# Second FFN of a four-layer token model on one core: dense experts against sorted token-expert tiles

## The chip, the core and the metric

The program runs on one core of a Trainium2 chip. The core has a matrix engine (TensorE, PE in the profile; PEld is its weight load), a vector engine (VectorE, DVE), an activation engine (ScalarE, ACT), a general engine (GpSimd, POOL) and a queue engine (SyncE, SP). They work on a memory of 128 partitions (SBUF); matmuls write to eight banks of PSUM, 128 x 512 floats each. The metric is the device time of one execution in microseconds (us), lower is better.

## The reference, cut to what matters

Eight images of 256 x 256 go through a wavelet step, an attention, a first FFN, a second attention and a second FFN. After the wavelet step there are 2304 tokens of 256 numbers. The second FFN is what the change touches:

```python
xf = layernorm(h)                                   # 2304 x 256
scores = sigmoid(xf @ gate_w.T + lb_bias)           # 2304 x 8
topw, topi = top_k(scores, 2); topw = topw / topw.sum(-1)
for e in range(8):
    m = topi == e; sel = m.any(-1)
    wmean = (topw * m).sum() / max(m.sum(), 1)      # one number for each expert
    y = mlp(xf, gate[e], up[e], down[e])            # 256 -> 128 -> 256, silu(g) * u
    out = out + where(sel, y * wmean, 0)
out = out + mlp(xf, shared_gate, shared_up, shared_down)   # 256 -> 256 -> 256
h = h + out
```

A token counts for two of eight experts, and all tokens for the shared one, which has twice the width and is handled as two halves of 128.

## The kernel before

The residual stream `h` stays in SBUF, 128 partitions x `NT` = 18 tiles x 256. Tokens go in `NG` = 6 groups of three tiles (`GW` = 384 tokens). Every matmul of the FFN is split in three: each float32 operand is a high part in the matmul's own format and a low rest, and high x high, low x high and high x low are added (`split3`, lines 1263 to 1265). The normalised tokens, transposed, lie as `xTh` and `xTl` (256 features x 2304 tokens), the weights as `W_h[1]` and `W_l[1]`; PS is PSUM.

The second FFN is `experts(1, 3)` on four engines. It is dense: ten experts (eight and the two shared halves) run over all six groups, 60 steps n. A step is, in order:

- PE `gate_up(n)`: 12 matmuls with 384 columns into banks 0/1 (gate) and 2/3 (up). It waits for `mul(n-2)`.
- ACT: `sg` = silu(gate) (line 660); DVE `gated(n)`: `aa` = `sg` x up (line 1095); ACT: `ah` = high part of `aa` (line 664); DVE `low(n)`: `al` = rest (line 1101).
- PE `down(n)`: nine matmuls with 256 columns. On PE's queue it stands behind `gate_up(n+1)`, so that the chain above runs beside that.
- DVE `accumulate(n)` (line 1116): three operations `h` = `h` + `cmb` x PSUM, where `cmb` is the expert's mean weight for a chosen token and 0 for another.

Ahead of it the router's logits are in bank 7; DVE's `compare(1)` and `weigh(1)` rank the eight scores of each token and count chosen tokens and weights over a partition (`tot`), PE adds these over the partitions with a matmul with ones (line 1433), and `average()` makes `cmb`. After each group's ten experts SP writes three tiles of `h` out (line 399). POOL has nothing to do in this stage. Each engine runs its own list of instructions in the order of the code, waits on semaphores, and nothing is rescheduled.

Ahead of the FFN a stage of six turns adds the attention's output to `h`, normalises it to `xnp` (two buffers, line 770) and transposes it.

## Time and profile before

| | us |
|---|---|
| median of three runs (881.36 to 884.1) | 882.18 |
| span of the profiled execution | 878.1 |
| attention, first FFN and all else up to the first matmul of the second FFN | 677.25 |
| second FFN, from there to the end of the span | 200.85 |

The profile is of one execution on the one core. Its span goes from the first to the last instruction; what lies around it in the measured time is the difference, 4.1 us against the median. Times within rows are from the span's start. The matmul rows overlap each other (each row's duration has the pipeline's latency in it), so the pace of matmuls is the distance of their starts, not their duration.

### The profile page before, as it was taken

The numbers are of one execution on the slowest core, as the hardware profiler recorded it, in microseconds if no ns is written. First come the engines' busy times: TensorE is split into PE (matmuls) and PEld (weight loads), VectorE is DVE, ScalarE is ACT, GpSimd is POOL, SyncE is SP. The second block draws the span as 40 slices with busy tenths as digits, with TensorE's granted clock in tenths as the row PEclk, the third lists the DMA queues.
The fourth block names the chain that finished last, engine by engine and source line by source line (L and its number), as shares of the span: only waits on it lengthen the run. The fifth ranks groups of instructions, "written<-read, shape, count | busy, mean of one in ns | idle before, by whom it ended". The sixth has DMA issues, their size and how long they took to land.

```text
span 878.1 us, 14320 instructions
## 1 busy us (share of the span) xinstructions
PE 735.0 (84%) x4732; PEld 617.8 (70%) x4732; DVE 614.6 (70%) x1388; ACT 346.6 (39%) x608; POOL 173.5 (20%) x143
## 2 busy tenths in 40 slices
PE   4008997889999999337999999999757899999997
PEld 1007996689999999226655555654545899999997
DVE  6497666677777777927676777673695777777776
ACT  0223554523333333110666666677246233333332
POOL 5623555000000000536112112211253000000000
...
GB/s 252 174 162 1 1 0 0 1 0 2 1 1 1 0 0 0 1 78 81 94 74 76 102 103 89 104 44 23 186 0 1 1 19 1 19 20 1 19 19 19
DMA packets 22246, 38.87 MB, mean 44 GB/s; under 512 B 6972, under 2 KB 17916, under 8 KB 21248
## 3 DMA queue, kind: packets, MB, share of 16 engines
...
q14 instruction: 23, 0.19, 0.1%
...
## 4 chain that ended last, share of the span: by engine, by line
PE 70%; DVE 14%; DMA 6%; issue 3%; ACT 3%; ACTq 2%; POOL 1%; SPq 1%; DVEq 0%; POOLq 0%
PE PS L1263 16%; PE PS L1265 16%; PE PS L1264 16%; PE PS L1541 6%; PE PS L1480 5%; PE PS L1498 4%; DMA wd<-in_wd 2%; DVE MX L1184 2%; DMA KS<-scrH 1%; DVE nmr L1250 1%; ACTq L549 1%; DVE stats L896 1%; PE PS L1323 1%; PE PS L1357 1%; DMA x_in<-in_x 1%
## 5 line engine op out<-in xcount | busy, mean ns | idle before, releaser
L1184 DVE TENSOR_REDUCE MX<-PS 128x1 f32<-128x288 f32 x288 | 125.1, 452 | 52.3 <-PE PS L1480 48.7
L1116 DVE SCALAR_TENSOR_TENSOR h<-PS,cmb,h 128x256 f32<-128x256 f32 (+1 forms) x342 | 143.7, 475 | 0.2 <-PE PS L1265 0.2
L692 ACT ACTIVATE PR<-PS 96x768 f32<-96x768 f32 x144 | 115.3, 806 | 47.8 <-PE PS L1498 44.7
L660 ACT ACTIVATE sg<-PS 128x384 f32<-128x384 f32 x114 | 55.9, 491 | 166.9 <-PE PS L1265 166.9
L1480 PE MATMUL PS<-KS,QS 96*128 96x288 f32 x288 | 97.7, 362 | 18.1 <-DMA KS<-scrH 15.9
L1101 DVE TENSOR_TENSOR al<-aa,ah 128x384 fp32r<-128x384 f32 x114 | 63.6, 558 | 67.2 <-ACT ah L664 67.2
L1480 PEld LDWEIGHTS PS<-KS,QS 96*128 96x128 f32 x288 | 57.6, 204 | 60.3 <-DVE MX L1184 38.7
L664 ACT ACTIVATE ah<-aa 128x384 fp32r<-128x384 f32 x114 | 60.0, 527 | 84.1 <-DVE aa L1095 84.1
L1095 DVE TENSOR_TENSOR aa<-sg,PS 128x384 f32<-128x384 f32 x114 | 63.3, 555 | 27.6 <-ACT sg L660 26.7
L1265 PE MATMUL PS<-xTl,W1h 128*128 128x384 f32 x240 | 81.0, 337 | 0.0
L1263 PE MATMUL PS<-xTh,W1h 128*128 128x384 f32 x240 | 80.8, 337 | 0.0
L1264 PE MATMUL PS<-xTh,W1l 128*128 128x384 f32 x240 | 80.7, 336 | 0.0
L1498 PE MATMUL PS<-QS,KS 128*96 128x384 f32 x288 | 75.9, 348 | 2.1 <-DVE MX L1184 1.1
L1263 PE MATMUL PS<-xTh,W0h 128*128 (+1 forms) x216 | 73.5, 340 | 0.0
L1265 PE MATMUL PS<-xTl,W0h 128*128 (+1 forms) x216 | 73.5, 340 | 0.0
L1264 PE MATMUL PS<-xTh,W0l 128*128 (+1 forms) x216 | 73.4, 340 | 0.0
L1541 PE MATMUL PS<-PR,VA 128*32 128x288 f32 x768 | 66.3, 418 | 1.1 <-ACT yr L746 1.0
L1263 PE MATMUL PS<-W1h,ah 128*128 128x256 f32 x180 | 51.2, 284 | 4.3 <-DVE al L1101 4.3
L1265 PE MATMUL PS<-W1l,ah 128*128 128x256 f32 x180 | 51.0, 283 | 0.0
L1264 PE MATMUL PS<-W1h,al 128*128 128x256 f32 x180 | 50.6, 281 | 0.0
L1263 PE MATMUL PS<-W0h,ah 128*128 128x256 f32 x162 | 46.5, 287 | 4.6 <-DVE al L1101 4.6
L1498 PEld LDWEIGHTS PS<-QS,KS 128*96 128x96 f32 x288 | 42.5, 166 | 9.9 <-ACT PR L692 4.8
...
## 6 DMA issues: line engine op xcount, KB each, us to landing
...
W1raw<-in_w SPq DMA_DIRECT2D x1, 3840.0 KB, 13.2
...
out_tokens<-h SPq DMA_DIRECT2D x6, 384.0 KB, 2.3
```

The lines of the kernel that those rows point to most:

```text
L664: A_(ah[:, b], aa[:, b], ACT.Copy).then_inc(s[f"f{L}_ah"], 1)
L692: A_(PR[0:KT, c0:c0 + 2, :], PS[0:KT, b:b + 2, 0:CW], ACT.Exp).then_inc(s["e_exp"], 1)
L1095: V.tensor_tensor(aa[:, b], sg[:, b], PS[:, 2 + b, 0:GW], ALU.mult).then_inc(s[f"f{L}_mul"], 1)
L1101: V.tensor_tensor(al[:, b], aa[:, b], ah[:, b].bitcast(F32), ALU.subtract).then_inc(s[f"f{L}_al"], 1)
L1116: ins = V.scalar_tensor_tensor(out=hj, in0=PS[:, b + t // 2, (t % 2) * D:(t % 2) * D + D], scalar=cmb[:, ds(g * GT + t, 1), e:e + 1].squee ...
L1184: V.tensor_reduce(MX[:, c // NSH, c % NSH:c % NSH + 1], PS[:, max_bank(it, c), 0:POS], AX_X, ALU.max).then_inc(s["e_mx"], 1)
L1263: M(out_, wh, xh, start=(start and c == 0), stop=False)
L1264: M(out_, wl, xh, start=False, stop=False)
L1265: ins = M(out_, wh, xl, start=False, stop=(stop and c == n - 1))
L1480: M(PS[:, max_bank(it, c), 0:POS], QS[q][0:MROW, c * P:c * P + P], KS[q][0:MROW, c // 9 * POS:c // 9 * POS + POS], start=True, stop=True). ...
L1498: ins = M(PS[0:KT, n % 4, 0:CW], KS[p][:, g * POS + kt * KT:g * POS + kt * KT + KT], QS[p][:, g * HQ + cc * CW:g * HQ + cc * CW + CW], sta ...
L1541: ins = M(PS[32 * hh:32 * hh + 32, 6, 0:POS], VA[p][:, kt, g, :], PR[:, c0:c0 + 3, :].rearrange("p c w -> p (c w)")[:, hh * POS:hh * POS + ...
```

## The change

The eight experts of the second FFN are no longer dense. A token has two chosen experts, so there are 4608 token-expert pairs. They are sorted by expert into tiles of 128 slots, each expert's last tile padded: `NTL` = 36 + 7 = 43 tiles always suffice and all 43 are run.

- While the first shared half (six dense steps) runs on PE, DVE works out the slot of each pair and from that the two index lists: `scan_counts`, `tile_bases`, `token_slots`, `one_hot_tiles`, `one_hot_rows` (three parts), `indices`, `tile_experts`. The lists are turned from slots by 36 matmuls of one-hot matrices between `gate_up(4)` and `down(2)`. `tile_experts` gives each tile's expert (PE loads these 43 numbers into registers and takes its weights by them) and the mean weight `wt`.
- In the stage ahead SP also writes `xnp` to the DRAM tensor `scrX`, six DMAs of 384 KB.
- Tile t: POOL gathers 128 rows of 1 KB from `scrX` with an indirect DMA into `xg` (four buffers); PE transposes them (`x_turn`, 2 matmuls), ACT and DVE make the high and low part (`x_high`, `x_low`), PE runs gate and up together with the tokens as weights (`a_gate_up`, 6 matmuls with 256 columns), ACT `a_silu`, DVE `a_gated`, PE `a_turn` (1 transpose), ACT `a_high`, DVE `a_low`, PE `a_down` (3 matmuls with 256 columns), ACT `y_out` (times `wt`, into `ysb`, four buffers), and POOL scatters the 128 rows into the DRAM tensor `scrY` by pair, with another indirect DMA.
- Then the second shared half runs (six dense steps), SP reads `scrY` back in six DMAs of 768 KB into `yb`, POOL adds the two rows of each token (`pair_sum`), DVE adds them and the shared half to `h` (`last_add`, `last_pair`), and SP writes `h` out at the end.
- In the dense steps the low part is made by POOL (`dense_low`), and the first half's result goes over ACT (`dense_out` to `ysh`) and POOL (`dense_add`) into `h`.
- Four small constant tables are loaded at the program's start by SP. Semaphores of the earlier stages are shared and get offsets; nothing else of these stages changes.

The core of the diff (the functions of the index lists are left out; their operations stand below by engine order):

```diff
+NTL = TOK * 2 // P + NE - 1
+NTP = (NTL + 1) // 2 * 2
+NXG, NXS, NYS = 4, 3, 4
+NDS = 2 * NG
...
-        with sp.Fori(0, NG) as g:
-            sp.wait_ge(s["f1_acc"], 10 * (g + 1))
-            sp.dma_start(out[:, ds(g * GT, GT), :], h[:, ds(g * GT, GT), :]).then_inc(s["d_out"], 16)
+        for g in range(NG):
+            sp.wait_ge(s["n_xn"], N0["p"] + g + 1)
+            sp.dma_start(scrX[g * GW:(g + 1) * GW, :].rearrange("(t p) d -> p t d", p=P), xnp[:, g % 2]).then_inc(s[f"d_xo{g % 2}"], 16)
+        for b in range(NYS):
+            sp.wait_ge(s[f"d_ys{b}"], 16 * len(range(b, NTL, NYS)))
+        for g in range(NG):
+            if g >= 4:
+                sp.wait_ge(s["m_ya"], g - 3)
+            sp.dma_start(yb[:, g % 4], scrY[2 * g * GW:2 * (g + 1) * GW, :].rearrange("(t p k) d -> p t (k d)", p=P, k=2)).then_inc(s[f"d_yb{g % 4}"], 16)
+        for g in range(NG):
+            sp.wait_ge(s["f1_out"], g + 1)
+            sp.dma_start(out[:, g * GT:(g + 1) * GT, :], h[:, g * GT:(g + 1) * GT, :]).then_inc(s["d_out"], 16)
...
+        def dense_low(n):
+            pool.wait_ge(s["f_ah"], F0[1, "ah"] + n + 1)
+            wait(pool, s["f_dn"], F0[1, "dn"] + n - 1)
+            nc.gpsimd.tensor_tensor(al[:, n % 2], aa[:, n % 2], ah[:, n % 2].bitcast(F32), ALU.subtract).then_inc(s["f_al"], 1)
+        def dense_add(n):
+            pool.wait_ge(s["f1_yc"], n + 1)
+            z = slice(n * GT, n * GT + GT)
+            nc.gpsimd.tensor_tensor(h[:, z, :], h[:, z, :], ysh[:, n % 2], ALU.add).then_inc(s["f_acc"], 1)
+        def gather(t):
+            wait(pool, s["m_xT"], t - NXG + 1)
+            nc.gpsimd.indirect_dma_start(xg[:, t % NXG, :], None, scrX, bass.IndirectOffsetOnAxis(ap=gix[:, t:t + 1], axis=0))\
+                .then_inc(s[f"d_xg{t % NXG}"], 16)
+        def scatter(t):
+            pool.wait_ge(s["m_yo"], t + 1)
+            nc.gpsimd.indirect_dma_start(scrY, bass.IndirectOffsetOnAxis(ap=six[:, t:t + 1], axis=0), ysb[:, t % NYS, :], None,
+                                         bounds_check=TOK * 2 - 1, oob_is_err=False).then_inc(s[f"d_ys{t % NYS}"], 16)
+        def pair_sum(g):
+            pool.wait_ge(s[f"d_yb{g % 4}"], 16 * (g // 4 + 1))
+            nc.gpsimd.tensor_tensor(yb[:, g % 4, :, 0:D], yb[:, g % 4, :, 0:D], yb[:, g % 4, :, D:2 * D], ALU.add).then_inc(s["m_ysum"], 1)
+        for n in range(NG):
+            dense_low(n)
+            if n >= 2:
+                dense_add(n - 2)
+        pool.wait_ge(s["m_idx"], 1)
+        pool.wait_ge(s["d_xo0"], 16 * (NG // 2))
+        pool.wait_ge(s["d_xo1"], 16 * (NG // 2))
+        gather(0)
+        gather(1)
+        dense_add(NG - 2)
+        dense_add(NG - 1)
+        for t in range(2, 5):
+            gather(t)
+        for t in range(NTL):
+            if t + 5 < NTL:
+                gather(t + 5)
+            scatter(t)
+        for n in range(NG, NDS):
+            dense_low(n)
+            if n >= NG + 2:
+                pair_sum(n - NG - 2)
+        pair_sum(NG - 2)
+        pair_sum(NG - 1)
...
+        def x_high(t):
+            act.wait_ge(s["m_xT"], t + 1)
+            wait(act, s["m_gu"], t - NXS + 1)
+            A_(xsh[:, t % NXS], PS[:, 6 + t % 2, 0:D].rearrange("p (k c) -> p k c", k=KC), ACT.Copy).then_inc(s["m_xh"], 1)
+        def a_silu(t):
+            act.wait_ge(s["m_gu"], t + 1)
+            wait(act, s["m_a"], t - 1)
+            A_(sgt[:, t % 2], PS[:, t % 2, 0:P], ACT.Silu).then_inc(s["m_silu"], 1)
+        def a_high(t):
+            act.wait_ge(s["m_aT"], t + 1)
+            wait(act, s["m_y"], t - 1)
+            A_(aht[:, t % 2], PS[:, 2 + t % 2, 0:P], ACT.Copy).then_inc(s["m_ah"], 1)
+        def y_out(t):
+            act.wait_ge(s["m_y"], t + 1)
+            wait(act, s[f"d_ys{t % NYS}"], 16 * (t // NYS))
+            A_(ysb[:, t % NYS], PS[:, 4 + t % 2, 0:D], ACT.Copy, scale=wt[:, t:t + 1]).then_inc(s["m_yo"], 1)
...
+        for i in range(NTL + 2):
+            if i < NTL:
+                a_silu(i)
+            if 1 <= i <= NTL:
+                a_high(i - 1)
+            if i + 2 < NTL:
+                x_high(i + 2)
+            if i >= 2:
+                y_out(i - 2)
+        for n in range(NG, NDS):
+            dense_silu(n)
+            dense_high(n)
...
+        compare(1)
+        weigh(1)
+        scan_counts()
+        gated(0)
+        tile_bases()
+        token_slots()
+        gated(1)
+        one_hot_tiles()
+        one_hot_rows(0)
+        gated(2)
+        one_hot_rows(1)
+        one_hot_rows(2)
+        gated(3)
+        indices()
+        tile_experts()
+        gated(4)
+        gated(5)
+        x_low(0)
+        x_low(1)
+        for i in range(NTL + 1):
+            if i < NTL:
+                a_gated(i)
+            if i >= 1:
+                a_low(i - 1)
+            if i + 2 < NTL:
+                x_low(i + 2)
+        for n in range(NG, NDS):
+            gated(n)
+            if n >= NG + 2:
+                last_add(n - 2)
+            if n >= NG + 3:
+                last_pair(n - NG - 3)
+        last_add(NDS - 2)
+        last_pair(NG - 3)
+        last_add(NDS - 1)
+        last_pair(NG - 2)
+        last_pair(NG - 1)
...
+        def x_turn(t):
+            pe.wait_ge(s[f"d_xg{t % NXG}"], 16 * (t // NXG + 1))
+            wait(pe, s["m_xl"], t - 1)
+            for k in range(KC):
+                ins = nc.tensor.transpose(PS[:, 6 + t % 2, k * P:k * P + P], xg[:, t % NXG, k * P:k * P + P], ident[:, :])
+            ins.then_inc(s["m_xT"], 1)
+        def a_gate_up(t, e):
+            pe.wait_ge(s["m_xl"], t + 1)
+            wait(pe, s["m_a"], t - 1)
+            o_ = PS[:, t % 2, 0:2 * P].rearrange("p (a i) -> p a i", a=2)
+            b = t % NXS
+            for k in range(KC):
+                M(o_, xsh[:, b, k], gu[0][:, :, ds(e + k * P, P)], start=(k == 0), stop=False)
+                M(o_, xsl[:, b, k], gu[0][:, :, ds(e + k * P, P)], start=False, stop=False)
+                ins = M(o_, xsh[:, b, k], gu[1][:, :, ds(e + k * P, P)], start=False, stop=(k == KC - 1))
+            ins.then_inc(s["m_gu"], 1)
+        def a_turn(t):
+            pe.wait_ge(s["m_a"], t + 1)
+            wait(pe, s["m_al"], t - 1)
+            nc.tensor.transpose(PS[:, 2 + t % 2, 0:P], aat[:, t % 2], ident[:, :]).then_inc(s["m_aT"], 1)
+        def a_down(t, e):
+            pe.wait_ge(s["m_al"], t + 1)
+            if t == 0:
+                pe.wait_ge(s["f1_yc"], NG)
+            wait(pe, s["m_yo"], t - 1)
+            o_ = PS[:, 4 + t % 2, 0:D]
+            b = t % 2
+            M(o_, aht[:, b], dn[0][:, ds(e, D)], start=True, stop=False)
+            M(o_, alt[:, b], dn[0][:, ds(e, D)], start=False, stop=False)
+            M(o_, aht[:, b], dn[1][:, ds(e, D)], start=False, stop=True).then_inc(s["m_y"], 1)
+        for n in range(NG):
+            dense_gate_up(n)
+            if n == 1:
+                pe.wait_ge(s["f1_tot"], 1)
+                M(PS[:, 7, 0:2 * NE], ones[:, :], tot[:, :], start=True, stop=True)
+                M(PS[:, 7, 2 * NE:3 * NE], tri[:, :], tot[:, 0:NE], start=True, stop=True).then_inc(s["f1_sum"], 1)
+            if n == 4:
+                for m in range(NT * 2):
+                    if m % (NT * 2 // 3) == 0:
+                        pe.wait_ge(s["m_oh"], m // (NT * 2 // 3) + 1)
+                    ins = M(PS[:, 6, 0:NTP], ohp[:, m], ohv[:, m], start=(m == 0), stop=(m == NT * 2 - 1))
+                ins.then_inc(s["m_ix"], 1)
+            if n >= 2:
+                dense_down(n - 2)
+        dense_down(NG - 2)
+        dense_down(NG - 1)
+        pe.wait_ge(s["m_te"], 1)
+        te = [pe.alloc_register(f"te{t}") for t in range(NTL)]
+        pe.load(te[0:22], tei[0:1, 0:22])
+        pe.load(te[22:NTL], tei[0:1, 22:NTL])
+        te = [pe.snap(r, min_val=0, max_val=(NE - 1) * KC * P) for r in te]
+        x_turn(0)
+        x_turn(1)
+        for i in range(NTL + 2):
+            if i < NTL:
+                a_gate_up(i, te[i])
+            if 1 <= i <= NTL:
+                a_turn(i - 1)
+            if i + 2 < NTL:
+                x_turn(i + 2)
+            if i >= 2:
+                a_down(i - 2, te[i - 2])
+        for n in range(NG, NDS):
+            dense_gate_up(n)
+            if n >= NG + 2:
+                dense_down(n - 2)
+        dense_down(NDS - 2)
+        dense_down(NDS - 1)
```

In the order lists that follow, a row is an instruction: line of the kernel, operation, output<-inputs, shape, and the semaphores that it waits for.

DVE at the start of the second FFN, before. `ra` are comparisons of scores, t_135 to t_137 the ranks and weights, `sv` the normed weights:

```order
L1045 TENSOR_TENSOR ra<-sc 128x18
L1095 TENSOR_TENSOR aa<-sg,PS 128x384 [waits f1_silu,dve_own]
L1101 TENSOR_TENSOR al<-aa,ah 128x384 [waits f1_ah]
L1050 TENSOR_REDUCE t_135<-ra 128x144
L1052 TENSOR_SCALAR t_136<-t_135 128x144 [waits dve_own]
L1054 TENSOR_TENSOR t_137<-t_136,sc 128x144 [waits dve_own]
```

And with the change, from the end of `token_slots` to the start of `indices`:

```order
L1504 CAST tpf<-tpi 128x72 [waits dve_own]
L1542 TENSOR_TENSOR aa<-sg,PS 128x384 [waits f_al,f_silu,dve_own]
L1509 TENSOR_TENSOR oht<-tpf,cst 128x1584
L1512 TENSOR_TENSOR ohv<-oht,vid 128x1584 [waits dve_own]
L1518 TENSOR_TENSOR ohp<-tpf,iot 128x1536 [waits dve_own]
L1542 TENSOR_TENSOR aa<-sg,PS 128x384 [waits f_al,f_silu]
L1518 TENSOR_TENSOR ohp<-tpf,iot 128x1536 x2
L1542 TENSOR_TENSOR aa<-sg,PS 128x384 [waits f_al,f_silu]
L1524 COPY ixf<-PS 128x43 [waits m_ix]
```

The gating of the first step (line 1095, now 1542) stood right behind the comparisons; now the gating operations of steps 0 to 5 stand spread over the whole index work, up to four of its large operations between two of them.

POOL after the last low part of the weights. Before, its list ends there:

```order
L413 TENSOR_TENSOR rstd<-mt,minus_half 128x3 [waits var_ready]
L537 TENSOR_TENSOR W1l<-W1raw,W1h 128x1280 [waits w_hi1]
L413 TENSOR_TENSOR rstd<-mt,minus_half 128x3 [waits var_ready]
L537 TENSOR_TENSOR W1l<-W1raw,W1h 128x1280 [waits w_hi1] x2
L1590 UNCONDITIONAL_BRANCH
```

With the change, from the last dense step of the first half on (rows of line 626 are gathers, of 632 scatters):

```order
L615 TENSOR_TENSOR al<-aa,ah 128x384 [waits f_dn,f_ah]
L621 TENSOR_TENSOR h<-h,ysh 128x768 [waits f1_yc]
L626 DMA xg<-scrX,gix 128x256 [waits d_xo1,d_xo0,m_idx]
L626 DMA xg<-scrX,gix 128x256
L621 TENSOR_TENSOR h<-h,ysh 128x768 [waits f1_yc] x2
L626 DMA xg<-scrX,gix 128x256 x2
L626 DMA xg<-scrX,gix 128x256 [waits m_xT] x2
L632 DMA scrY<-ysb,six 4608x256 [waits m_yo]
L626 DMA xg<-scrX,gix 128x256 [waits m_xT]
L632 DMA scrY<-ysb,six 4608x256 [waits m_yo]
L626 DMA xg<-scrX,gix 128x256 [waits m_xT]
L632 DMA scrY<-ysb,six 4608x256 [waits m_yo]
```

So gather t+6 stands right behind scatter t on one in-order queue, and scatter t waits for `y_out(t)`.

PE in the experts' part, before (the last three of a dense step's 12 gate-and-up matmuls and the first three of the nine `down` matmuls behind them):

```order
L1263 MATMUL PS<-xTh,W1h 128x384
L1264 MATMUL PS<-xTh,W1l 128x384
L1265 MATMUL PS<-xTl,W1h 128x384
L1263 MATMUL PS<-W1h,ah 128x256 [waits f1_acc,f1_al]
L1264 MATMUL PS<-W1h,al 128x256
L1265 MATMUL PS<-W1l,ah 128x256
```

With the change, the end of one tile turn (after its six gate-and-up matmuls, of which the last three stand here) and the first row of the next:

```order
L1997 MATMUL PS<-W1h,xsh 128x256
L1998 MATMUL PS<-W1h,xsl 128x256
L1999 REGISTER_ALU
L1999 MATMUL PS<-W1l,xsh 128x256
L2006 MATMUL PS<-ident,aat 128x128 [waits m_al,m_a]
L1987 MATMUL PS<-ident,xg 128x128 [waits m_xl,d_xg1]
L1987 MATMUL PS<-ident,xg 128x128
L2016 ISA [waits m_al]
L2016 MATMUL PS<-W1h,aht 128x256
L2017 MATMUL PS<-W1h,alt 128x256
L2018 REGISTER_ALU
L2018 MATMUL PS<-W1l,aht 128x256
```

In turn i PE runs the gate and up of tile i, the inner transpose of tile i-1, the transpose of the gathered rows of tile i+2 (it waits for that gather's landing, `d_xg1` here) and the down matmuls of tile i-2.

## Rows read from the trace of the kernel before

**Rows 1.** The page: busy time by engine; DMA rate in 40 slices of the span.

```profile
PE 735.0 (84%) x4732; PEld 617.8 (70%) x4732; DVE 614.6 (70%) x1388; ACT 346.6 (39%) x608; POOL 173.5 (20%) x143
...
GB/s 252 174 162 1 1 0 0 1 0 2 1 1 1 0 0 0 1 78 81 94 74 76 102 103 89 104 44 23 186 0 1 1 19 1 19 20 1 19 19 19
```

**Rows 2.** Timeline of the second FFN, its ends: start, duration, engine, line, operation.

```profile
677.25 0.44 PE L1263 MATMUL PS<-xTh,W1h 128*128 128x384 f32 x1
...
872.55 0.38 PE L1263 MATMUL PS<-W1h,ah 128*128 128x256 f32 x1 [1.25 <-DVE al L1101]
...
875.37 0.34 SPq L399 DMA_DIRECT2D out_tokens<-h  x1
```

**Rows 3.** The same view, one dense step and a pair of its down matmuls.

```profile
775.96 0.34 PE L1263 MATMUL PS<-xTh,W1h 128*128 128x384 f32 x1
...
778.17 0.28 PE L1264 MATMUL PS<-W1h,al 128*128 128x256 f32 x1
...
778.29 0.28 PE L1265 MATMUL PS<-W1l,ah 128*128 128x256 f32 x1
...
779.13 0.34 PE L1263 MATMUL PS<-xTh,W1h 128*128 128x384 f32 x1
```

**Rows 4.** Busy time by stretch, 720 to 875 us: length, PE, PEld, DVE, ACT, POOL, clock.

```profile
720.00:875.00 155.00, 152.63 (x1012) 152.22 (x1010) 112.45 (x247) 48.87 (x96) 0.00 (x0) 1.00 0.03 12
```

**Rows 5.** Timeline, DVE's router work at the start of the second FFN.

```profile
678.58 0.31 DVE L1045 TENSOR_TENSOR ra<-sc 128x144 f32<-128x144 f32 x1 [0.92 <-ACT sc L650]
...
680.96 0.55 DVE L1095 TENSOR_TENSOR aa<-sg,PS 128x384 f32<-128x384 f32 x1
...
686.14 0.40 DVE L1071 TENSOR_REDUCE tot<-sv 128x8 f32<-128x144 f32 x1
```

**Rows 6.** Groups by shape on DVE: line, output<-inputs, shapes, count | busy us, mean ns.

```profile
L1095 DVE TENSOR_TENSOR aa<-sg,PS 128x384 f32<-128x384 f32 x60 | 33.3, 555 | 16.7 <-ACT sg L660 16.1 <-DVE tot L1071 0.5
L1239 DVE TENSOR_TENSOR h<-PS,h 128x768 f32<-128x768 f32 x6 | 5.7, 950 | 4.3 <-PE PS L1570 4.3
L1067 DVE TENSOR_TENSOR sv<-t,t 128x144 f32<-128x144 f32 x1 | 0.3, 309 | 0.0
```

**Rows 7.** Groups by shape on ACT, as in rows 6.

```profile
L746 ACT ACTIVATE yr<-PS 128x288 f32<-128x288 f32 x32 | 13.0, 406 | 1.0 <-PE PS L1541 1.0
L709 ACT ACTIVATE VA<-PS 96x64 f32<-96x64 f32 x24 | 3.5, 220 | 0.5 <-PE PS L1512 0.5
```

**Rows 8.** Groups by shape on POOL, as in rows 6.

```profile
L450 POOL TENSOR_TENSOR qs<-qsq 128x384 f32<-128x384 f32 x6 | 6.0, 1004 | 43.9 <-ACT qsq L591 43.9
L464 POOL TENSOR_TENSOR a1l<-a1raw,a1h 128x768 fp32r<-128x768 f32 x1 | 1.9, 1902 | 4.8 <-ACT a1h L671 4.8
L413 POOL TENSOR_TENSOR rstd<-mt,minus_half 128x3 f32<-128x3 f32 x6 | 5.1, 855 | 25.8 <-DVE mt L798 25.8
L438 POOL TENSOR_TENSOR rwl<-rw,rwh 128x16 fp32r<-128x16 f32 x2 | 3.5, 1777 | 0.0
```

**Rows 9.** The DMA view: tensors, issuing queue, count, KB each, us to landing.

```profile
recb<-scrR ACTq DMA_DIRECT2D x56, 36.0 KB, 1.9
...
W1raw<-in_w SPq DMA_DIRECT2D x1, 3840.0 KB, 13.2
...
out_tokens<-h SPq DMA_DIRECT2D x6, 384.0 KB, 2.3
```

**Rows 10.** Timeline, six transposes at full clock.

```profile
117.74 0.82 PE L1292 MATMUL PS<-ident,xn 128*128 128x128 f32 x6
```

**Rows 11.** Busy time by stretch of 4 us, as in rows 4 (PE first, clock third from the end).

```profile
640.00:644.00 4.00, 0.07 (x1) 0.08 (x2) 3.72 (x14) 3.44 (x5) 0.91 (x2) 0.87 0.00 0
644.00:648.00 4.00, 4.00 (x14) 2.83 (x15) 3.97 (x3) 1.14 (x3) 2.80 (x1) 0.50 0.00 0
684.00:688.00 4.00, 2.54 (x15) 2.12 (x13) 3.22 (x12) 0.37 (x1) 0.00 (x0) 1.00 0.00 2
```

**Rows 12.** The chain that ended last, at the program's start: start, length, what.

```profile
21.86 21.89 DMA wd<-in_wd
```

337 lines of the change are left out of this document (276 added, 61 removed).

## Prediction

> **What bounds the kernel now.** I read the page's busy line first, then the timeline of the second FFN, then its groups. PE is busy 84% of the span [rows 1], and in the stretch that the change rewrites it never rests: from 720 to 875 us it is busy 152.6 of 155 us at full clock, DVE 112 us, ACT 49 us, POOL not at all [rows 4]. One dense step takes 779.13 - 775.96 = 3.17 us of PE [rows 3]; DVE's and ACT's work of a step is shorter and lies beside it. 60 steps make 190 us of the 200.85 us from the first gate matmul at 677.25 to the end of the span at 878.1 [rows 2]; the rest is router work at the head and the last chain and store at the end. So matmul columns bound this stage, and the change removes columns: 48 of 60 dense steps, 48 x 3.17 = 152 us. What it puts there is bound by other things, and the question is by what.
>
> **The work of a tile.** Matmuls of 256 columns start 0.12 us apart (778.17, 778.29) [rows 3]; a transpose of 128 columns takes about 0.11 us ((0.82 - 0.16) / 6 [rows 10]; 0.16 is what a matmul's duration has over its distance, 0.28 - 0.12 [rows 3]). A tile has nine such matmuls and three transposes: 9 x 0.12 + 3 x 0.11 = 1.4 us of PE at full clock, 60 us for 43 tiles. ACT has two operations of 128 and two of 256 columns. Between 64 columns (220 ns) and 288 (406 ns) a column costs 0.83 ns [rows 7], so these take 0.27 and 0.38 us, 1.3 us in all. DVE has two of 128 and one of 256: between 144 (309 ns) and 384 (555 ns) it is 1.0 ns a column [rows 6], 0.3 + 0.3 + 0.42 = 1.0 us. Each chain is staggered over turns. If nothing but these engines counted, a turn would be about 1.5 to 1.6 us, half of a dense step, though 43 turns replace 48 steps.
>
> **POOL and the transfers set the turn.** A turn also has one gather and one scatter on POOL's in-order queue. The trace has no indirect DMA. Its nearest rows bound what POOL spends on one, D. From below it is SP's issue of a plain 128-partition transfer, 0.34 us [rows 2]. From above I take the longest of POOL's small operations, 1.78 us for 16 columns; the power on three columns takes 0.86 us [rows 8]. Working out 128 addresses is a loop on this engine like these, not a fixed issue like SP's, so I take the mean of 0.86 and 1.78, **D = 1.3 us**. From issue to landing a plain transfer takes 1.9 us for 36 KB from DRAM and 2.3 us for 384 KB to it [rows 9]; for 128 KB I take 2.1 less the issue, 1.8 us after POOL is done.
>
> Now the loop. Gather t+6 stands behind scatter t, scatter t waits for `y_out(t)`, that for the down matmuls at the end of PE's turn t+2; and gather t+6 must have landed for `x_turn(t+6)` in PE's turn t+4. So two turns hold: 0.6 us from PE's last matmul to the end of `y_out` (0.2 latency, 0.38), 2D = 2.6 for scatter and gather, 1.8 for the landing, 0.6 for the transposes and the down matmuls that end turn t+4. That is 5.6 us, **2.8 us a turn**. POOL's own bound, 2D = 2.6, is just under it; PE's 1.4 is hidden. Four buffers for gathered rows and four for results don't bind earlier: in 4 x 2.8 us both transfers are long over. In general the turn is T = max(2D, D + 1.5).
>
> The Trainium skill (DMA: Bandwidth & Descriptors, Anatomy of one DMA) puts a GpSimd-issued transfer at 2.0 us and its bytes over 436 GB/s, 2.3 us here from end to end; with that instead of D + 1.8 a turn would come to 2.4 us (0.6 + 1.3 for the scatter + 2.3 + 0.6, halved) and the total 14 us lower. No transfer of this kind is in this trace.
>
> **The head, 677.25 to 730 us.** Without the change DVE does the comparisons from 678.58, gates step 0 at 680.96, and ends the weighing at about 686.5 [rows 5]. Now comparisons (2.4 us), weighing (4.0) and the scan (0.7) stand ahead of `gated(0)`, which ends at 686.2; PE can run only two gate-and-ups ahead and stands. Behind it DVE has `tile_bases` (2.2 us: nine operations of 0.16 to 0.31 us with waits between them), `token_slots` (2.3), a gating (0.56), five one-hot operations of 1536 or 1584 columns (1.8 each by 1.0 ns a column and 0.2, so 9.0), two gatings, the wait for PE's last 12 index matmuls (1.3), `indices` (1.5) at 703.6, `tile_experts` (3.0) and the last gatings to 707.7. PE then has the last down matmuls, whose low parts come from POOL at 1.0 us each [rows 8]: done at about 712. This is 35 us for six dense steps that take 19 on their own: 16 us of index work that nothing covers. The indices are ready at 703.6 but POOL reaches gather 0 only behind the low part of step 5 and an add of 768 columns (1.9 us) [rows 8], at 711.6; two gathers (2.6), two more adds (3.8), then gathers 2, 3, 4 at 1.3 each, and the transposed rows of tiles 2 to 4 come one by one as they land, 721 to 724. Scatter 0 and gather 6 follow at 726.2 and 727.5, and turn 4 ends at **730**. So the head, with turns 0 to 4 in it, takes 53 us.
>
> **The loop.** Turns 5 to 40 wait for gathers: 36 x 2.8 = 101 us. The last four wait for none: 1.5 each, 6 us. It ends at 837.
>
> **The tail.** Six dense steps at 3.17 are 19 us, and the last gating, high part, low part (on POOL now) and down matmuls stand alone: before, PE idled 1.25 us ahead of them at 872.55 and they ran 1.2 [rows 2]; with POOL and its waits 3.5 us in all. Then a `last_add` and two `last_pair` at 0.95 [rows 6] and the store, 2.7 us from 875.37 to the end [rows 2]: 28 us. Beside it run the last scatters (landed 3.4 us behind the last turn) and six loads of 768 KB. 3840 KB take 13.2 us [rows 9], so one takes 2.6 at that pace, the last lands at 20.5, its pair sum (1.9), add and store end at 26. This is just hidden; 10% slower loads would show. End at 865.
>
> **Small parts.** The stage ahead writes `xnp` to DRAM: a 384 KB store lands in 2.3 us [rows 9] and a buffer comes round only each second group, so nothing waits; SP has nothing urgent behind it. If it were not hidden it would cost at most 2.3 us a group, 14 us. At the start SP gets four more loads, 290 KB, that share the engines with weight loads on the chain, `wd` to 43.75 us [rows 12]: about 1.2 us at the 252 GB/s of the first slice [rows 1]. That half of `h`'s updates now go over ACT and POOL costs nothing: both have under 3 us a step of 3.17.
>
> **Sum.** 865 + 1.2 = 866 us of span against 878.1, 12 us less. Around the span lie 4.1 us (882.18 - 878.1), kept: **870 us**.
>
> **Rivals.**
> - *POOL's queue becomes the bound and loses more than PE gains* (slower). Head and tail are fixed, so the change breaks even at T = 2.8 + 12 / 36 = 3.1 us; by T = max(2D, D + 1.5) from D = 1.6 us on. At the row of 1.78 us it is 3.56, 27 us above the forecast: 897 us. For it: the upper row is a plain operation on far less data. Against: the pow row. Chance 0.20.
> - *Cheap issues.* With D = 0.7, twice SP's issue [rows 2], T is 2.2 and the end 36 x 0.6 = 22 us earlier: 848 us. At D = 0.34 the bound is 1.84 and the total 835. Chance 0.19.
> - *The clock falls in the loop.* After a stretch with 0.07 us of PE work in 4 us the granted clock went to 0.50; with 2.54 of 4 us it stayed at 1.00 [rows 11]. PE stands nearly idle from 712 to 721, so the tiles start at half of 2.4 GHz, where a turn is 2.8 us of PE and no longer hidden; at 1.4 of 2.8 us busy it may stay there, which adds the doubled transposes and downs to the loop: (5.6 + 0.6) / 2 = 3.1 us a turn, 11 us more, no gain left, 881 us. That row's busy share, 64%, lies above the loop's 50%, so this is open. Chance 0.13.
> - *Gathers and scatters don't overlap* (slower). If each must land before the next is served, a turn is 2 x (1.3 + 1.8) = 6.2 us: 36 x 3.4 = 122 us more, 992 us. Nothing in the code orders the two kinds, so this has 0.03. The Trainium skill speaks for large transfers (DMA: Bandwidth & Descriptors, Rules for kernel authors: at least 1 MiB per DMA; under 64 KB mostly overhead); these are 128 KB.
>
> **Chances and range.** The forecast, D from 1.1 to 1.5 and with it T from 2.6 to 3.0, has 0.45 and spans 862 to 878 us. Faster by over 0.3% (under 879.5; 0.3% is about what a measurement tells from no change) are the forecast, the cheap issues and a third of the clock's case: 0.68. Within 0.3% are the rest of the clock's case and a little of the first rival: 0.10. Slower: 0.22. The range reaches from D = 0.5 (T = 2.0, 841) to T = 3.45 (893): 840 to 893 us.
>
> **What would show it right or wrong.** In the changed kernel's trace: starts of `a_gate_up` 2.8 us apart and PE's waits in `x_turn` ended by the DMA into `xg`; POOL's DMA rows near 1.3 us; turn 4 over at 730, first gather at 711 to 712, loop's end at 837; PE stopped behind line 1542 in the head. If PE's waits are ended by POOL's queue with no gap on POOL, it is the 2D bound; if POOL's rows are 1 us or less, the cheap case. The forecast is wrong if a first use of the indirect DMA costs more than the later ones, or if `yb` loads of 2 KB rows are slower than weight loads.

## Result

The changed kernel takes 904.53 us (median of 4 runs, 903.03 to 910.2) where the one before takes 881.85: ratio 1.0254, 95% interval 1.0224 to 1.0283. Forecast were 870 us, range 840 to 893, slower with 0.22. It is slower, by 23 us, and outside the range. The profiled execution has a span of 903.7 us, 37.5 more than my sum of 865 + 1.2.

The page of the changed kernel, answering to [rows 1]:

```profile
PE 688.0 (76%) x4278; PEld 557.6 (62%) x4278; DVE 555.4 (61%) x1276; ACT 358.7 (40%) x690; POOL 298.5 (33%) x253
...
PEclk9999999899999998566999999998968677888787
...
PE 52%; DVE 17%; DMA 12%; issue 7%; POOL 5%; ACT 4%; ACTq 1%; SPq 1%; DVEq 0%; POOLq 0%
```

The same two lines of the kernel before, the clock and the chain of work that ended last:

```profile
PEclk9999998889999999556899999999978999999999
...
PE 70%; DVE 14%; DMA 6%; issue 3%; ACT 3%; ACTq 2%; POOL 1%; SPq 1%; DVEq 0%; POOLq 0%
```

PE has 47 us less to do than before, and the span is 26 us longer: what left the matmuls came back as DMA and "issue" in the chain, and TensorE's granted clock is lower in the last quarter. The stage in stretches of 15 us (length, PE, PEld, DVE, ACT, POOL, clock), answering to [rows 4]:

```profile
745.00:760.00 15.00, 9.22 (x58) 8.00 (x58) 4.15 (x14) 6.05 (x20) 9.33 (x10) 0.84 0.24 76
760.00:775.00 15.00, 12.59 (x57) 11.06 (x56) 4.14 (x13) 5.96 (x18) 8.64 (x9) 0.51 0.24 75
775.00:790.00 15.00, 7.91 (x58) 6.70 (x57) 4.36 (x15) 6.29 (x20) 9.85 (x10) 1.00 0.26 84
```

No engine is full, and the stretch at half clock (0.51) gets about as many matmuls done (57) as the one at full clock (58). So PE's work does not set the loop's time, though its clock has a share in it, told of below. The chain of waits shows whose it is. One round of it (start, length, what):

```profile
844.62 0.48 ACT ysb L941
845.10 0.02 issue
845.13 0.03 POOLq L632
845.15 0.74 issue
845.90 1.02 POOL scrY L632
846.91 0.31 issue
847.22 2.72 DMA xg<-scrX,gix
849.94 0.04 issue
849.99 0.69 PE PS L1987 x2
850.67 0.21 PE PS L2016
850.89 0.21 PE PS L2017
851.10 0.23 PE PS L2018
851.33 0.02 issue
851.35 0.48 ACT ysb L941
```

This is the cycle that the prediction described: `y_out(t)`, scatter t, gather t+6, its landing, `x_turn(t+6)`, the down matmuls, `y_out(t+2)`. It takes 851.35 - 844.62 = 6.73 us for two turns, 3.36 a turn, where I had 5.6 and 2.8. From gather 6 (740.5) to gather 42 (861.6) the 36 turns took 3.36 us each.

### The profile page after: what moved, and what is told of

Read it like the earlier page. It is cut to its first block, busy times and chain, and to the rows that moved or that the text cites. A ratio compares the mean times of both kernels' runs of the same rounds, so it can differ in the third digit from the quotient of the medians.

```text
span 903.7 us, 13928 instructions
## 1 busy us (share of the span) xinstructions
PE 688.0 (76%) x4278; PEld 557.6 (62%) x4278; DVE 555.4 (61%) x1276; ACT 358.7 (40%) x690; POOL 298.5 (33%) x253
## 4 chain that ended last, share of the span: by engine, by line
PE 52%; DVE 17%; DMA 12%; issue 7%; POOL 5%; ACT 4%; ACTq 1%; SPq 1%; DVEq 0%; POOLq 0%
PE PS L1627 9%; PE PS L1629 9%; PE PS L1628 9%; DMA xg<-scrX,gix 6%; PE PS L1905 6%; PE PS L1844 5%; PE PS L1862 4%; DMA wd<-in_wd 3%; POOL scrY L632 2%; DVE MX L1372 2%; DMA KS<-scrH 2%; PE PS L1987 1%; DVE nmr L1438 1%; DVE stats L1084 1%; ACTq L674 1%
## 5 line engine op out<-in xcount | busy, mean ns | idle before, releaser
L1304 DVE SCALAR_TENSOR_TENSOR h<-PS,cmb,h 128x256 f32 (+1 forms) x162 | 68.1, 475 | 0.0
L1987 PE MATMUL PS<-ident,xg 128*128 128x128 f32 x86 | 23.8, 372 | 55.6 <-DMA xg<-scrX,gix 48.4
L1547 DVE TENSOR_TENSOR xsl<-PS,xsh 128x256 fp32r<-128x256 f32 x43 | 18.3, 425 | 72.4 <-ACT xsh L923 72.3
L584 POOL TENSOR_TENSOR recb<-yr,recb 128x1152 f32<-128x1152 f32 x7 | 18.5, 2650 | 128.5 <-DMA recb<-scrR 128.5
L632 POOL DMA_INDIRECT scrY<-ysb,six x43 | 43.6, 1015 | 48.1 <-ACT ysb L941 40.5
L785 ACT ACTIVATE sg<-PS 128x384 f32<-128x384 f32 x54 | 26.5, 491 | 79.1 <-PE PS L1629 79.1
L1987 PEld LDWEIGHTS PS<-ident,xg 128*128 128x128 f32 x86 | 11.5, 179 | 65.1 <-DMA xg<-scrX,gix 57.7
L1289 DVE TENSOR_TENSOR al<-aa,ah 128x384 fp32r<-128x384 f32 x54 | 30.2, 558 | 32.1 <-ACT ah L789 32.1
L626 POOL DMA_INDIRECT xg<-scrX,gix x43 | 42.1, 980 | 12.8 <-issue 11.0
L1629 PE MATMUL PS<-W0l,ah 128*128 128x256 f32 x162 | 45.9, 283 | 0.0
```

The lines of the kernel that those rows point to most:

```text
L626: nc.gpsimd.indirect_dma_start(xg[:, t % NXG, :], None, scrX, bass.IndirectOffsetOnAxis(ap=gix[:, t:t + 1], axis=0))\
L632: nc.gpsimd.indirect_dma_start(scrY, bass.IndirectOffsetOnAxis(ap=six[:, t:t + 1], axis=0), ysb[:, t % NYS, :], None, bounds_check=TOK * 2 ...
L1304: ins = V.scalar_tensor_tensor(out=hj, in0=PS[:, b + t // 2, (t % 2) * D:(t % 2) * D + D], scalar=cmb[:, ds(g * GT + t, 1), e:e + 1].squee ...
L1629: ins = M(out_, wh, xl, start=False, stop=(stop and c == n - 1))
L1987: ins = nc.tensor.transpose(PS[:, 6 + t % 2, k * P:k * P + P], xg[:, t % NXG, k * P:k * P + P], ident[:, :])
```

## Where the 37.5 us are

| piece | predicted | measured | difference |
|---|---|---|---|
| first gate matmul | 677.25 + 1.2 | 679.42 | +1.0 |
| from there to the end of turn 4 | 52.8 | 64.9 (744.3) | +12.1 |
| to the last down matmul | 107 | 125.9 (870.2) | +18.9 |
| to the end | 28 | 33.5 | +5.5 |

**Loop.** The two waits of the cycle, PE's in `x_turn` for the landing and POOL's for `y_out`, from 725 to 850 us (total, times, longest). The forecast had both; they are longer than it had them:

```profile
PE PS L1987 <- DMA xg<-scrX,gix: 43.0, 27, 3.4
POOL scrY L632 <- ACT ysb L941: 32.1, 20, 4.8
```

**Head.** Rows of the timeline, PE, DVE, POOL and PE again:

```profile
687.29 0.61 PE L2024 MATMUL PS<-tot,ones 128*128 128x16 f32 x2 [3.44 <-DVEq L1261]
...
712.07 0.20 DVE L1524 COPY ixf<-PS 128x43 f32<-128x43 f32 x1 [7.20 <-PE PS L2030]
...
723.48 1.19 POOL L626 DMA_INDIRECT xg<-scrX,gix  x1 [0.18 <-issue]
...
730.10 1.11 PE L1987 MATMUL PS<-ident,xg 128*128 128x128 f32 x4 [6.98 <-issue]
```

PE pauses 3.44 us for the totals and 2.6 us ahead of `gate_up(4)`; the clock is 0.50 from 700 to 716 us, so that step takes 4 us and the 36 index matmuls 7.7 us (0.214 apart). The lists are ready at 713.4, forecast 703.6; gather 0 starts 10.1 us behind them, forecast 8.0; and then 7.0 us of PE go to two reads of 22 and 21 registers (the expert offsets, 2.05 and 4.99 us), for which the sum had no term. Counted from the first gate matmul, the 12.1 us over the forecast are 7.6 to the lists, 2.1 from there to gather 0, 1.1 from gather 0 to scatter 0 (15.7 for 14.6) and 1.3 on to turn 4.

**Tail.** Groups from 870 us on, DVE's and POOL's, answering to [rows 6, 8] (after the bar busy us, then mean ns):

```profile
L1575 DVE TENSOR_TENSOR h<-yb,h 128x768 f32<-128x768 f32 x6 | 10.1, 1684 | 1.0 <-POOL yb L638 0.6 <-DVE h L1575 0.2
L1568 DVE TENSOR_TENSOR h<-PS,h 128x768 f32<-128x768 f32 x6 | 5.7, 956 | 0.3
...
L638 POOL TENSOR_TENSOR yb<-yb 128x768 f32<-128x768 f32 x6 | 13.7, 2300 | 0.0
```

and the loads of the pairs, on the page:

```profile
yb<-scrY SPq DMA_DIRECT2D x6, 768.0 KB, 6.1
```

An addition of 768 columns takes DVE 950 ns and POOL 1.9 us alone [rows 6, 8]; with both at work on such additions the mean is 1684 and 2300 ns. Only `last_pair` (L1575, both inputs in SBUF) is slower; `last_add` (L1568, one input in PSUM) stays at 956 ns in the same stretch. A load takes 6.1 us to land, but the next ones run beside it: POOL never stood idle ahead of a sum (0.0), and the last additions wait for POOL's sums and not for a load.

## Experiments

The experiments ran in five groups on five chips, A to E, each chip once. The ratio is always to the kernel before, run beside the others of its group, with its 95% interval. No ratio of the kernels with a lead of 6 or 7 is more than 2% from 1. Where a time stands against one of another chip, the text says so.

### The cycle, by the lead of the gathers

`gather(t + L)` is started ahead of `scatter(t)`; L is 5 in the change. The gather behind scatter t is t+L+1, needed L-3 turns after `y_out(t)`: the cycle's time is spread over L-3 turns.

```
-            if t + 5 < NTL:
-                gather(t + 5)
+            if t + 7 < NTL:
+                gather(t + 7)
```

Lead 7 (chip A) and lead 4 (chip B):

> GpSimd starts gather t+7 instead of gather t+5 ahead of scatter t; nothing else changes. Theory A (the loop runs at a cycle: y_out(t), GpSimd's start on scatter t, gather t+6 behind it, its landing, two tiles later in x_turn): with seven tiles of lead the landing no longer stands in the cycle, the turn falls from 3.36 us toward GpSimd's own two issues with their gaps (1.02 + 0.30 + 0.98 + 0.30 = 2.60 us), the 43 us of waits of x_turn on the gathered rows nearly vanish, and the time falls by about 25 us, to 880. Theory B (the gathers' transfers themselves are slow or the clock sets the turn): the wait stays at x_turn, with later landings, and the time stays within 3 us of the change's.

> The gathers run four tiles ahead in place of five. Cycle theory: one round of y_out, scatter, gather, landing, x_turn to y_out, which spans L - 3 turns at a lead of L (two at 5, over which it measured 6.2 to 6.7 us), now has to fit into one turn: the turn goes from 3.36 to 6.2 to 6.7 us, and the time up by 36 to 38 turns times 3.0 us, to 1010 to 1030. Rival (the loop is bound by transfers, by the clock or by the engines' work in it, and the lead only smooths it): less than 40 us more.

Lead 6 (chip D), after the pauses told of below had been seen:

> The changed kernel with a lead of six as the one edit. Cycle theory: the round of 6.2 to 6.7 us now spans three turns, 2.1 to 2.2 us each, under GpSimd's 2.60, so the turn is 2.60 and the time that of the lead of seven, 870 to 880, if ScalarE makes no pauses. If pauses of ScalarE (1 to 3 us with nothing that the trace shows to wait for, 43 us in all) are the rule once GpSimd's queue runs without a gap, they appear here, and the time is 890 to 900.

| lead | turns in the cycle | us a turn | time, ratio |
|---|---|---|---|
| 4 | 1 | 6.87 | 1041.3, 1.1788 (1.1764 to 1.1811) |
| 5 | 2 | 3.36 | 904.5, 1.0254 |
| 6 | 3 | 2.61 | 877.2, 0.9923 (0.9886 to 0.9960) |
| 7 | 4 | 2.60 | 874.7, 0.9911 (0.9877 to 0.9945) |

At lead 4 the round of the chain is the same 6.77 us, in one turn:

```profile
903.07 0.48 ACT ysb L941
...
904.35 1.01 POOL scrY L632
...
905.67 2.76 DMA xg<-scrX,gix
...
909.84 0.48 ACT ysb L941
```

Half of 6.73 is 3.36; a third would be 2.24, but POOL alone needs 2.60 for a scatter and a gather with the 0.30 us behind each, and from lead 6 on its DMAs follow each other at that distance nearly throughout. Timeline of POOL at lead 7:

```profile
765.48 0.98 POOL L626 DMA_INDIRECT xg<-scrX,gix  x1 [0.30 <-issue]
766.76 1.02 POOL L632 DMA_INDIRECT scrY<-ysb,six  x1 [0.30 <-issue]
768.09 0.97 POOL L626 DMA_INDIRECT xg<-scrX,gix  x1 [0.31 <-issue]
```

Theory A holds: the cycle cost the loop its gain. With the same DMAs and the same work, two tiles sooner in the queue, `x_turn(0)` to the last down matmul takes 107.5 us in place of 140.1, and the kernel comes under the one before, on this chip. (The medians are 30 us apart, across two chips. In that profile the lists were also ready 3.1 us sooner, by the clock in the index matmuls; more of this below.)

### The clock

```
+            wait(pe, s["m_xl"], t - 1)
+            for _ in range(3):
+                M(PS[:, 6 + t % 2, 0:P], ones[:, :], ident[:, :], start=True, stop=True)
             pe.wait_ge(s[f"d_xg{t % NXG}"], 16 * (t // NXG + 1))
-            wait(pe, s["m_xl"], t - 1)
```

> Three idle matmuls of 128 columns are put ahead of each x_turn's wait for its gathered rows, into the columns that the transposes then write; they fill some 0.6 us of the pause of each turn. If the half clock of parts of the loop (mean 0.76 over 730 to 860) is a cause of the long turns of its own, the granted clock rises to about 1 and the turn falls from 3.36 to about 3.1 us, 9 us less in all. If the cycle through GpSimd and the transfer sets the turn whatever the clock, the time changes by under 3 us either way.

```profile
805.00:820.00 15.00, 10.40 (x81) 9.38 (x79) 4.14 (x14) 5.67 (x18) 8.95 (x9) 1.00 0.25 74
```

907.4 us, 1.0280 (1.0249 to 1.0312). The clock was 0.93 to 1.00 from 745 on and the round 6.25 us where it closes (840.75 to 847.00), yet gathers were 3.32 us apart on the mean: a scatter also waits at times behind a gather of POOL's own queue. So at full clock too the loop is far over the forecast's 2.8. The run does not settle the clock's own share, since the added matmuls stand in PE's queue themselves and delay a turn whose rows have landed. The change's own trace bounds it: from 775 to 790 (clock 1.00) four gathers follow at 3.12 us each, from 760 to 775 (clock 0.51) at 3.49. Against the mean of 3.36 the half clock costs up to 0.24 us a turn, an estimate of at most 9 us of the loop.

In the head, with twelve and eight such matmuls in PE's two pauses:

> Twelve idle matmuls in TensorE's pause ahead of the totals (685 to 688) and eight in the one ahead of gate_up(4) (697 to 700). Theory: the half clock of 700 to 715 costs 2 us in gate_up(4) and 3.9 us in the 36 index matmuls, so the lists are ready 5 to 6 us sooner; but gather 0 starts 10 us behind the lists, held by GpSimd's dense_low and adds, so that the kernel gains 3 to 6 us. Rival: an index matmul is bound by its weight load and its interval of 0.214 us stays at full clock; then 2 us or less.

903.3 us, 1.0222 (1.0184 to 1.0261). The clock was 1.00 from 700 to 708 us and the index matmuls took 4.1 us in place of 7.7, so the rival on the weight load falls; first gate matmul to `x_turn(0)` is 46.8 us where it was 50.7. The median moved by 1.2 us, inside both intervals, so that no gain in the time is shown. Nor is the shorter head shown to be the edit's: of the 17 other profiles with the index work, none of them with this edit, ten have the 36 index matmuls in 4.6 to 5.2 us and seven in 7.7, with both kinds on chip B. Lead 4 and lead 7 have 46.9 and 47.5 us to `x_turn(0)` with the head as in the change. The clock of this stretch differs from one execution to another, by some 3 us of the head.

### The head's other pieces

Offsets read one per turn, behind `a_gate_up(i)`, in the change (chip A) and at lead 7 (chip D):

```
-        pe.load(te[0:22], tei[0:1, 0:22])
-        pe.load(te[22:NTL], tei[0:1, 22:NTL])
+            if i + 1 < NTL:
+                pe.load(te[i + 1:i + 2], tei[0:1, i + 1:i + 2])
```

> TensorE reads the expert offset of tile i+1 behind gate_up(i), one register at a time, in place of two reads of 22 and 21 registers ahead of the loop (2.05 and 4.99 us). Theory: gather 0 has landed at 726.5 and x_turn(0) starts at 730.1, so 3.6 us are gained and the loop is unchanged: minus 3.6 us. Rival: each single read costs about a microsecond on TensorE's sequencer in each of the 43 turns; where the pause of the turn hides it, minus 3.6 stays, where not, up to 20 us more.

906.8 us, 1.0252 (1.0219 to 1.0285): nothing gained. Gather 0 to `x_turn(0)` fell from 6.6 to 3.0 us, but to scatter 0 only from 15.7 to 14.6, and the loop from `x_turn(0)` was 2 us longer: turns 2 to 4 wait for gathers that POOL starts late, so that of the 3.6 us some 1.1 stood on the path. That profile's stage ahead also ended 8.6 us later.

> On the kernel with a lead of seven: expert offsets read one per turn, as the one edit. There the two reads stand at the path (dense_down(5) ends at 719.5, x_turn(0) starts at 726.5, gather 0 has landed at 722.8). Theory: x_turn(0) 3.7 us sooner, loop at GpSimd's 2.60 us as before: 871. Rival: this kernel falls into ScalarE's pauses as the five others with a lead of seven: 890 or more; then the one without pauses was the exception and not the order of GpSimd's queue.

870.9 us, 0.9868 (0.9801 to 0.9936). First gate matmul to `x_turn(0)`: 43.4 us, where 47.5 had stood. The medians are 3.8 us apart, across two chips, and that this is the number expected is luck: from `x_turn(0)` to the last down matmul it took 110.6 us for 107.5, so that from the first gate matmul 1.0 us is left of it (154.0 for 155.0), and 3.5 of the 4.4 us between the two spans lie ahead of the second FFN.

Lists that are not computed (the output is another; what is left out stands in the expectation), lead 7, chip C:

> On the kernel with a lead of seven: the counting, the slots, the one-hots, the 36 index matmuls and the tiles' experts are left out; gather and scatter lists are the tokens in order, the expert offset is that of expert 0, and the pair weight 0.5, so the output is another. Everything else stays. Theory (the head's length is that of the list building): VectorE's 15 us of it and the 5 to 8 us of index matmuls go, the dense steps follow each other at about 3.2 us from 687 on, x_turn(0) starts at 706 to 710 in place of 726.5, and the time falls by 17 to 20 us, to 855 to 858. Rival (GpSimd's dense_low and adds, 2.8 us a step and stretched, and the 7 us of register loads set the start): 5 us or less.

884.8 us, 1.0013 (0.9991 to 1.0035), on a chip where lead 7 has the pauses told of next. First gate matmul to `x_turn(0)` is 35.9 us against 47.5 and 50.7 in the two profiles of lead 7: building the lists costs 12 to 15 us on the path, under the 17 to 20 expected, since behind the last dense step the 7.0 us of reads still stand. Against lead 7 with the pauses (1.0101, chip E) the ratio is 0.9 points lower, 8 us.

Gathers 0 and 1 ahead of `dense_low(4)`:

> On the kernel with a lead of seven: gathers 0 and 1 are put ahead of dense_low(4) and (5) in GpSimd's order. In that kernel gather 0 starts 10.3 us behind the last step of the lists. Theory A (the head is late by GpSimd's order): gather 0 starts 1 us behind the lists, but dense_low(4) now waits for the lists too (they are there at 710, dense_low(4) ran at about 715), so nothing is lost there, x_turn(0) starts as soon as TensorE has done dense_down(5) and its register loads, 3 to 5 us sooner: 870. Theory B (x_turn(0) is held by TensorE's dense steps and the 7 us of register loads behind them): within 1.5 us of 874.7.

> Gathers 0 and 1 ahead of dense_low(4) and (5), lead of seven, once more; it had the pauses and took 891. If they belong to the chip, it stands against the lead of seven as the edit alone does: within 1.5 us of it if TensorE's dense steps and register loads hold x_turn(0), 3 to 5 us under it if GpSimd's order does.

On chip B 891.0 us, 1.0069 (1.0034 to 1.0105). On chip E, beside lead 7 without the edit, 894.1 us, 1.0110 (1.0071 to 1.0149), against 894.5; first gate matmul to `x_turn(0)` 50.8 against 50.7: no gain. Theory B holds: 10 us between the lists and gather 0 look long, but `x_turn(0)` waited for PE's own steps and reads.

### The same kernel, 20 us apart on two chips

The run on chip B took 891.0, not 870 to 875, and the next with a lead of 7, on chips B and C, were slow as well. In these, ACT starts operations up to 3.1 us late: ACT's groups, lead 7 on chip A, and the same kernel on chip E (idle time ahead, and what ended it):

```profile
L941 ACT ACTIVATE ysb<-PS,wt 128x256 f32<-128x256 f32 x31 | 14.7, 474 | 0.8 <-PE PS L2018 0.7
L929 ACT ACTIVATE sgt<-PS 128x128 f32<-128x128 f32 x31 | 8.6, 277 | 9.4 <-PE PS L1999 9.4
```

```profile
L941 ACT ACTIVATE ysb<-PS,wt 128x256 f32<-128x256 f32 x27 | 12.9, 479 | 16.3 <-remote 10.3 <-PE PS L2018 5.2 <-issue 0.8
L929 ACT ACTIVATE sgt<-PS 128x128 f32<-128x128 f32 x27 | 7.6, 281 | 20.9 <-PE PS L1999 10.8 <-remote 7.8 <-issue 2.4
```

I call it a pause where an ACT operation starts over 0.3 us after both its PE operation and its predecessor have ended. Summed over the loop, the pauses are 0 to 0.7 us in all profiles at lead 4 or 5 (chips A, B, C among them) and on chips A and D at lead 6 or 7, and 55 to 59 us, 39 to 48 pauses, in the eight at lead 7 on chips B, C and E. Gathers that land long ahead of the loop are one suspect, tried at lead 5:

> The changed kernel itself, lead of five, with gathers 0 and 1 ahead of dense_low(4) and (5) as the one edit. It asks where the pauses of ScalarE come from that lengthened the loop from 107 to 126 us when this edit was made at a lead of seven. If they come with early gathers: ScalarE's unexplained pauses (43 us in all there) appear here too, and the time is 910 or more. If they need GpSimd's queue without a gap (lead of seven): none of them, and 900 to 905.

Chip C: 909.1 us, 1.0275 (1.0256 to 1.0295), no pauses; it is not the early gathers alone. The next two ask for the lead and for the landings that ACT waits for, both on the kernel with two dense steps ahead of the loop, told of below:

> The kernel of the two dense steps ahead of the loop, with a lead of six in place of seven. If ScalarE's pauses hang on how far GpSimd may run ahead, they shrink and the time falls from 888 toward 868; if they hang on a queue without a gap, 885 to 890.

> The kernel of the two dense steps ahead of the loop, lead of seven, with eight output tiles instead of four, so that y_out(t) waits for the landing of scatter t-8 and not t-4. If ScalarE's pauses are waits for landings of scatters, they go and the time falls to about 868; if not, 885 to 890.

Both ran without pauses on chip D, 874.8 us, 0.9874 (0.9815 to 0.9934) and 868.5 us, 0.9834 (0.9766 to 0.9902), and so did the two others on that chip (lead 6, and lead 7 with reads per turn): four kernels without pauses tell nothing of the edits, and point to the chip. By then ten kernels at lead 6 or 7 had run, five with pauses and five without (the next expectation counts one fewer with them). Three kernels unchanged on chip E decide it, of which one had run without pauses and two with:

> The lead of seven once more, unchanged, beside the next two on one chip. So far the eight runs of kernels with a lead of six or seven fall in two groups: five without ScalarE's pauses on two chips (loop 104 to 108 us from x_turn(0) to the last down), four with 43 to 49 us of them on two other chips. If the pauses belong to the chip, the three kernels here are all with, or all without; without them this one comes to 875 again, with them to about 893.

> The kernel of the two dense steps ahead of the loop once more, unchanged; it had the pauses and took 888. If they belong to the kernel, 885 to 890 here whatever the lead of seven beside it does; if to the chip, the same group as the lead of seven: 868 without, 888 with.

Lead 7 unchanged: 894.5 us, 1.0101 (1.0066 to 1.0136), with pauses of 58 us, turn 3.08 us. Two steps: 895.2 us, 1.0119 (1.0087 to 1.0151). The pauses go with the chip (or with what else differed between the five groups, since no chip was used twice) and with POOL's queue at its limit: chips B and C had none at lead 4 and 5. A piece of the timeline of lead 7 on chip E, PE's last gate-and-up matmul of tile 6, and ACT's silu of that tile with the operation before it:

```profile
744.58 0.28 PE L1999 MATMUL PS<-W1l,xsh 128*128 x1
...
745.93 0.47 ACT L941 ACTIVATE ysb<-PS,wt 128x256 f32<-128x256 f32 x1 [0.39 <-remote]
748.81 0.28 ACT L929 ACTIVATE sgt<-PS 128x128 f32<-128x128 f32 x1 [2.40 <-PE PS L1999]
```

What ACT waits for there can be read from the semaphores' updates in the traces. 335 of the 343 pauses end within 0.06 us behind an update of the very semaphore that the tile's own PE operation raises, and none behind a landing that the operation waits for. For tile 6 above the matmul has ended at 744.86 by its row and the update comes at 748.78, 3.9 us later; in the profiles without pauses at lead 6 and 7 it always comes 0.02 us behind the row's end. So ACT does not wait for scatters to land, which the run with eight output tiles, made where no pauses were, could not tell; it waits for PE's signal. Whether the matmul itself ends late (the ends of PE's rows are modelled) or only its signal is late, and why on some chips alone, stays open. At lead 5, where POOL's queue has gaps, chips A and C gave 903 to 909 us.

### The tail, and moving the dense steps

All six dense steps of the second half ahead of the loop, and then in addition both additions of a pair sum on DVE (lead 7, reads per turn, chip B, with pauses):

> On the kernel with a lead of seven, with the offsets read one per turn: the six dense steps of the second shared half move from behind the loop to ahead of it. Theory (the head has 20 to 25 us in which TensorE only waits for the lists, and the tail of 33.5 us is TensorE's 19 us of dense steps beside 17.5 us of transfers at the 400 GB/s that its windows show): the head ends at about 727 in place of 726.5, and the tail shrinks from 33.5 to some 20 us (2 landing of the last scatter, 3 first pair load, 12 to 14 for six pair sums on GpSimd and VectorE, 3 last store): about 860. Rival: VectorE, busy without a break to 704 and with 9.5 us more work (gated and last adds) in the head, pushes the loop's start back by the full 19 us; then 874 or more.

> On the kernel of the shared halves ahead of the loop: VectorE does both additions of a pair sum, and GpSimd none. In the changed kernel's tail GpSimd's pair_sum took 2.30 us and VectorE's last_pair 1.68 us beside it, where such an operation of VectorE alone took 0.95. Theory (the two engines hold each other up over their two inputs): six times 2 x 0.95 = 11.4 us in place of 6 x 2.3 = 13.8 and the 1.7 behind the last, 3 to 4 us less. Rival (the tail then goes by its loads of 768 KB, 4.6 MB at 400 GB/s = 11.5 us): within 1 us.

```profile
L1562 DVE TENSOR_TENSOR yb<-yb 128x768 f32<-128x768 f32 x6 | 5.8, 958 | 11.2 <-DMA yb<-scrY 10.0 <-DVE h L1564 1.2
L1564 DVE TENSOR_TENSOR h<-yb,h 128x768 f32<-128x768 f32 x6 | 5.8, 958 | 0.2
```

902.0 us, 1.0197 (1.0173 to 1.0221), and 901.3 us, 1.0200 (1.0149 to 1.0252). From the last down matmul of the loop to the end the first takes 30.7 us, the second 26.0, with 33.5 in the change: alone, DVE's additions are back at 958 ns, and the 4.7 us are somewhat more than the 3 to 4 expected, though the medians (0.7 apart) don't show them. The steps ahead of the loop gave back 2.8 us in the tail and pushed `x_turn(0)` back by 16.8 us: it starts 60.2 us behind the first gate matmul, where the same kernel with the steps behind the loop has 43.4. The rival, which had the full 19 us, was nearly right. Two steps in place of six, in the 7 us that PE spent on reads:

> On the kernel with a lead of seven: two of the six dense steps of the second half go into TensorE's pause ahead of the loop (7 us there), offsets are read one per turn, four gathers instead of two are started ahead of the last two adds, and VectorE does the pair sums alone. Expected from the rows: loop start as before at about 726.5 (6.4 us of dense work in place of 7.0 us of register loads), the tail 33.5 - 6.4 = 27 us: 868. Rival (the pauses of up to 3 us of ScalarE that stood in the loops with early gathers, 42 us in all, come with any gather that lands long ahead of the loop): 885 or more.

Chip C, 887.7 us, 1.0076 (1.0037 to 1.0114), with pauses. With eight output tiles in place of four, on chip D, it gave the lowest median, 868.5 us, against 870.9 for lead 7 with reads per turn on the same chip: the intervals of the two ratios overlap, so neither is shown to be the faster, and the profiles say why (tail 28.9 in place of 33.6 us, head 48.6 in place of 43.4).

So five versions beat the kernel before on chips A and D, by 0.8 to 1.7%, with every interval under 1. The one of them that was run again elsewhere, lead 7, was 1.0% slower than the kernel before on chip E. None is shown to be faster on every chip.

## Why the prediction was wrong

- **What sets the turn: right.** PE waits in `x_turn`, ended by the DMA into `xg`; POOL has gaps; the cycle has the steps that were named, and the three other leads bear out its form.
- **Its size: wrong, and this is the step that failed.** At full clock a round is 6.25 us, at half clock 6.73, not 5.6. I set D = 1.3 and it is 0.98 and 1.02, so the dear term was cheap (2 D = 2.0 for 2.6), and issue to landing is 2.75 where D + 1.8 gave 3.1. (The estimate of 2.3 us worked out from the Trainium skill, DMA: Bandwidth & Descriptors, Anatomy of one DMA, is 0.45 short. The turn of 2.4 us made from it also lies under the forecast's own bound of 2D = 2.6; by that bound it would have been 7 us less in all, not 14.) What was missing has no busy time in any row of before: 0.80 us from the end of `y_out` to POOL's start on the scatter, 0.31 between two of POOL's DMAs, and 0.85 to 1.34 us of PE in place of 0.6. T = max(2D, D + 1.5) took D for all that POOL does; right is max(2D + 0.6, cycle / (L - 3)). Over the 36 turns the 0.56 us are 20 of the 37.5 us, about 12 of them at full clock already (3.12 for 2.8).
- **Luck.** POOL's own bound came out right, 2.60 us at leads 6 and 7 for 2D = 2.6: a D that was 0.3 too large stood for the gap of 0.3 that the sum had left out.
- **The rivals.** "POOL bound" had the right sign and the wrong cause: D never came near 1.6. But its break-even, a turn of 3.1 us, was passed: the turn was 3.36. The clock did fall, with a round 0.48 us longer (the forecast 0.6); this is the rest of the 20 us, at most 9, and alone it would have left 879 us. Holding it up gained nothing that the time shows. Cheap issues were true of D, and no help.
- **Head: 12 us over.** The half clock in the index matmuls (7.7 us for 4.1) and in `gate_up(4)` (2 us), two of five one-hots stretched beside POOL's low parts and adds (2.5 us each for 1.8), and the 7 us of register reads, of which 3.6 stood beyond the landing and about 1 on the path. I had named the index work as uncovered and costed each piece at its undisturbed row. (The forecast's own pieces add up to lists at 704.2, not 703.6, and in the tail its last load at 19.2, not 20.5; neither matters.)
- **Tail: 5.5 us over.** Additions of DVE and POOL were costed alone, and each ran beside the other. The Trainium skill (GPSIMD Engine Reference, Specifications) says that GpSimd shares its SBUF interfaces with VectorE and contends with instructions that have two SBUF inputs; the trace agrees: 958 ns with VectorE alone at work (the run above), 1684 beside GpSimd, and 956 in the same stretch for the addition that has one input in PSUM.
- **The range** took its width from D. The other terms of the cycle had none, though they came from rows of another kind of transfer.
